# Another order for the last six down products of each batch, and a split end for the last store, in an AdaLN attention and LoRA-expert kernel

## What is computed

```python
g, u = xf @ Wg.T, xf @ Wu.T                       # 1024 x 704
base = silu(g) * u @ Wd.T                         # the base unit
for e in experts:                                 # rows outside the top two have weight 0
    h = silu(g + xf @ Ag_e.T @ Bg_e.T * 2) * (u + xf @ Au_e.T @ Bu_e.T * 2)
    acc += h @ Ad_e.T @ Bd_e.T * 2 * w_e
x = x + gb * (base + acc)
```

## Time and profile before

| | |
|---|---|
| median of 3 runs | 710.68 us (710.49 to 711.01) |
| profiled execution, its own time | 710.4 us |
| its span in the trace | 708.6 us |
| TensorE / VectorE / GpSimd / ScalarE busy | 94% / 72% / 55% / 48% |
| granted TensorE clock, mean | 0.992 |

### The profile page before, as it was taken

How to read it: one execution, slowest core, us unless ns; L and a number is a source line. 1 busy time by engine, 2 the same in 40 slices (tenths; PEclk the granted TensorE clock), 3 DMA queues, 4 the chain that set the end, 5 groups by cost and what they waited for, 6 DMA issues and landing times.

```text
span 708.6 us, 10697 instructions
## 1 busy us (share of the span) xinstructions
PE 665.5 (94%) x3760; PEld 561.0 (79%) x3760; DVE 509.1 (72%) x1152; ACT 340.2 (48%) x604; POOL 392.2 (55%) x518
## 2 busy tenths in 40 slices
PE   5879999999999999999999999999999999999995
PEld 3669977877789987877788897887778997788884
DVE  5996786688976778578986678677988669536323
ACT  4534354535355345454355436364445535454542
POOL 3794457537772257456774238554775245743644
PEclk9989999999999999999999999999999999999999
DMA  8400010000000010000000002000000000000000
GB/s 303 117 1 1 1 61 1 0 1 31 0 2 31 1 61 1 0 1 31 0 1 31 1 1 61 0 1 1 30 2 1 31 1 1 0 1 1 31 0 31
DMA packets 14037, 15.44 MB, mean 22 GB/s; under 512 B 1312, under 2 KB 12704, under 8 KB 13984
## 3 DMA queue, kind: packets, MB, share of 16 engines
q1 hardware_dynamic: 13984, 14.76, 6.4%
HBM read 10.57 MB, written 4.19 MB: 21 GB/s over the span
## 4 chain that ended last, share of the span: by engine, by line
PE 55%; DVE 28%; issue 9%; POOL 5%; ACT 2%; DMA 1%; POOLq 0%; SPq 0%; DVEq 0%; ACTq 0%
PE ps L1198 50%; PE ps L1207 5%; DVE hid L1068 4%; DVE zb L799 3%; DVE zb L817 3%; POOL ring_lo L441 2%; DVE zb L804 2%; DVE stat L814 1%; DVE tm_hi L1058 1%; DVE tm_lo L1058 1%; DVE xr L817 1%; DMA xs<-in_L_attn_x 1%; DVE onehot L1019 1%; DVE stat L951 1%; DVE mv L791 1%
## 5 line engine op out<-in xcount | busy, mean ns | idle before, releaser
L441 POOL TENSOR_TENSOR ring_lo<-hid,ring_hi 128x512 fp32r<-128x512 f32 x144 | 192.3, 1342 | 104.2 <-ACT ring_hi L684 103.4
L676 ACT ACTIVATE act_s<-ps 128x512 f32<-128x512 f32 x120 | 71.8, 599 | 150.3 <-PE ps L1198 150.3
L1068 DVE TENSOR_TENSOR hid<-act_s,ps 128x512 f32<-128x512 f32 x120 | 81.5, 681 | 78.7 <-ACT act_s L676 69.5
L684 ACT ACTIVATE ring_hi<-hid 128x512 fp32r<-128x512 f32 (+1 forms) x144 | 90.3, 627 | 18.9 <-DVE hid L1068 10.2
L429 POOL TENSOR_TENSOR xr<-xr,xs 128x256 f32<-128x256 f32 x32 | 23.4, 733 | 91.8 <-DVE xr L959 91.8
L1198 PE MATMUL ps<-wdT_hi,ring_hi 128*128 128x256 f32 x192 | 53.1, 282 | 0.0
L1198 PE MATMUL ps<-wdT_lo,ring_hi 128*128 128x256 f32 x192 | 52.5, 279 | 0.0
L1198 PE MATMUL ps<-xT_hi,wgT_hi 128*128 128x512 f32 x96 | 39.3, 409 | 8.1 <-DVE hid L1068 8.1
L631 ACT ACTIVATE pT_hi<-ps 128x512 fp32r<-128x512 f32 (+3 forms) x48 | 21.8, 488 | 47.8 <-PE ps L1207 47.5
L1198 PE MATMUL ps<-wdT_hi,ring_lo 128*128 128x256 f32 x160 | 44.6, 279 | 0.0
L1198 PE MATMUL ps<-tm_hi,bgT_hi 128*128 128x512 f32 x96 | 40.6, 423 | 3.4 <-DVE hid L1068 3.3
(11 more groups left out here) (219 smaller groups left out, 2074.6 us busy)
## 6 DMA issues: line engine op xcount, KB each, us to landing
xs<-in_L_attn_x SPq DMA_DIRECT2D x4, 1024.0 KB, 5.6
out<-xr SPq DMA_DIRECT2D x7, 512.0 KB, 2.9
s_mod<-in_L_wmod SPq DMA_DIRECT2D x1, 1024.0 KB, 8.8
s_qkvT<-in_L_attn_qkv SPq DMA_DIRECT2D x1, 768.0 KB, 10.5
s_wg<-in_L_ffn_Wg SPq DMA_DIRECT2D x1, 704.0 KB, 8.0
s_wu<-in_L_ffn_Wu SPq DMA_DIRECT2D x1, 704.0 KB, 9.4
s_wd<-in_L_ffn_Wd SPq DMA_DIRECT2D x1, 640.0 KB, 8.3
s_mod<-in_L_wmod SPq DMA_DIRECT2D x1, 512.0 KB, 6.8
```

What stands on the lines that cost most here:

```text
L441: pool.tensor_sub(ring[1][:, place(n), :], hid[:, n % HID, :], ring[0][:, place(n), :].bitcast(fp32)).then_inc(h_lo.sem, 1)
L676: nc.scalar.activation(act_s[:, n % 2, :], ps[:, 2 * (n % 2), :], ACT.Silu).then_inc(silu_ready.sem, 1)
L684: nc.scalar.activation(ring[0][p0:P, place(n), :], hid[p0:P, n % HID, :], ACT.Copy).then_inc(h_hi.sem, 1)
L1068: V.tensor_mul(hid[:, n % HID, :], act_s[:, n % 2, :], ps[:, 2 * (n % 2) + 1, :]).then_inc(h_ready.sem, 1)
```

## The change

Two edits. First, `down_order` gives the last group of the last chunk, in every batch, the order expert one, expert two, base. Before, it had base, expert one, expert two. The transposes of the next batch keep their position: ahead of the first and of the second of the six. Second, in the last batch only: the eighth tile of `xr` is added by VectorE and no longer by GpSimd, and the last four tiles are stored as two, one and one, where they were stored as two and two.

```diff
         def down_order(ci, g):
-            slots = (0, 1, 2) if ci or g else (1, 2, 0)
+            slots = (1, 2, 0) if (ci, g) in ((0, 0), (NC - 1, GROUPS - 1)) else (0, 1, 2)
...
-        LAST_PIECES = 2
+        LAST_PIECES = ((TC, TC + 1), (TC + 2,), (TC + 3,))
...
-                    n = TC // LAST_PIECES if last and ci == NC - 1 else TC
-                    for i in range(ci * TC, (ci + 1) * TC, n):
-                        sp.wait_ge(out_ready.sem, out_ready.at(b, i + n - 1))
+                    pieces = LAST_PIECES if last and ci == NC - 1 else (range(ci * TC, (ci + 1) * TC),)
+                    for piece in pieces:
+                        i, n = piece[0], len(piece)
+                        if last and i == NT - 1:
+                            sp.wait_ge(last_row, 1)
+                        else:
+                            sp.wait_ge(out_ready.sem, out_ready.at(b, i + n - 1))
...
-                out_rows(b, range(TC, NT))
+                out_rows(b, range(TC, NT - 1 if last else NT))
...
                         V.tensor_mul(y_gb[:, t % 2, :], ...).then_inc(y_scaled.sem, 1)
+                        if last and i == NT - 1:
+                            dve.wait_ge(y_scaled.sem, y_scaled.at(b, i))
+                            V.tensor_add(xr[:, i, :], xr[:, i, :], y_gb[:, t % 2, :]).then_inc(last_row, 1)
```

More of the change, by code:

```diff
@@ L196, in adaln_attention_moe_lora @@
         unwaited = sem("unwaited")
+        last_row = sem("last_row")
         def signal(name, per_batch, credit=0):
@@ L362, in body @@
                 for ci in range(NC):
-                    n = TC // LAST_PIECES if last and ci == NC - 1 else TC
-                    for i in range(ci * TC, (ci + 1) * TC, n):
-                        sp.wait_ge(out_ready.sem, out_ready.at(b, i + n - 1))
+                    pieces = LAST_PIECES if last and ci == NC - 1 else (range(ci * TC, (ci + 1) * TC),)
[5 more added lines that the diff above has]
+                            sp.wait_ge(out_ready.sem, out_ready.at(b, i + n - 1))
                         sp.dma_start(out[b, i * P:(i + n) * P, :].rearrange("(i p) d -> p i d", p=P), xr[:, i:i + n, :]).then_inc(stored, 16)
             batches(sp, body)
-            sp.wait_ge(stored, 16 + 16 * (NC * B + LAST_PIECES - 1))
+            sp.wait_ge(stored, 16 + 16 * (NC * B + len(LAST_PIECES) - 1))
         @block.gpsimd
```

## The result

The changed kernel takes 714.21 us (median of 5, 714.09 to 714.47) against 710.68 us: ratio 1.0048, 95% interval 1.0034 to 1.0063. It is slower by half a per cent. The forecast was 714.2 us.

What follows compares the result with a forecast made beforehand. TensorE, 94% busy and without slack at the seams, was taken as the bound; the end chain runs through other engines. +4.1 + 0.0 - 0.65 = +3.5 us gave a 714.2 us median, range 713.3 to 715.3.

Steps and rivals of the forecast that it cites:

- The seams: At the three passages to the next batch, TensorE stands still: +1.38 us each, +4.1 us together.
- the slow start in the middle of the queries: At 211.06 us queries waited for split inputs of the second half; coming later they no longer wait: -0.13 us.
- The first stall: Ahead of the second transposes, TensorE waits for VectorE's last two normalised tiles: 0.8 us, where 12 base matmuls ran.
- the second: Ahead of the last expert down, TensorE waits for ScalarE's stack: 0.7 us, where 8 base matmuls ran.
- The last batch: Order in the final batch: stack and TensorE arrive together, so the last expert down starts no sooner; gain 0.0 us.
- The end: Last tile and stores: last store issued 0.26 us sooner, landing 0.4 us shorter; -0.65 us.
- the line through two rows: Last store's landing: 2.9 us at 512 KB and 2.1 at 256 KB, so 1.7 estimated at 128 KB.
- held-up add: VectorE's add of the last tile taking 1.40 us, the worst of its kind, with no shorter landing: bound +0.6 us.
- A: Rival: the order pays in the last batch and is free between batches; 708.0 us, chance 0.02.
- B: Rival: the passages between batches absorb the stall fully; 710.0 us, chance 0.05.
- C: Rival: another engine's wait in the attention part absorbs half of the stall; 712.0 us, chance 0.09.
- D: Rival: shifted queries meet another engine's queue, each batch losing some 0.8 us more; 716.5 us, chance 0.07.

Runs made afterwards that it cites:

- the pair of runs with VectorE's low part: New adds and stores, VectorE making unit 35's low part in GpSimd's place in the last batch: old order 710.19 us, new order there 709.20 us.
- the order alone: Kernel before with only the new order of the last downs in all four batches, its adds and stores unchanged: 714.47 us, ratio 1.0055.
- the single-stores run: Kernel before with only the last two tiles stored singly, old order, all four last adds on GpSimd: 710.26 us, ratio 0.9997.

## Why the prediction was right

**The seams, 1.38 us each, 4.1 in all: right by its own steps.** The second transposes at their old time, the stack at its old time, the first query 1.51 us later, the slow start in the middle of the queries gone: each stands in the trace; the stretches grew by 1.41, 1.30 and 1.45. That the median came out at 714.21, 0.01 from the forecast, is luck: the profiled spans differ by 3.7 us and not 3.5, and single executions of a kernel scatter by 0.4 us and more. The step on which it rested, that nothing in ScalarE's order depends on what moved, is shown by the stack's time in the trace after, and by the run that moves it. That all of it arrives at the end is shown by the first up product, 4.16 us later beyond the 0.11 of the start.

The first stall was put at 0.8 us with work missing from it, the second at 0.7; recorded are 0.64 and 0.55, since the record counts the wait from the end of a matmul and I counted from where the next could have started. The sum did not go by them. But I had not seen that they are coupled: filling the first makes the second vanish as well, though the rows that tell it, the stack's end and the rates of the downs, were all in my sum.

**The last batch, 0.0 us: right for the wait, silent on the clock.** The stack and TensorE's arrival coincide, as read from 697.98 and 698.09; the pair of runs with VectorE's low part shows both bounds. What I left out was that the filled idle time can also keep the clock at 2.4 GHz. The profile of before did not show it, since its clock held. It is worth 0.5 us (6.76 against 6.25) in the executions in which the clock falls as late as in that trace, more than my bounds of 0.1; in the medians, 709.81 against 710.04, it is not told from nothing. It may be why the order alone cost 3.8 us in the medians while its three stretches grew by 4.0, and why the change cost 3.5 us in the medians and 3.7 in the profiled spans; that is not shown.

**The end, -0.65 us: right, 0.59 measured.** The last issue came 0.29 us sooner, counted from the first up product (4.02 against 4.31), where 0.26 was worked out, and 0.1 us after VectorE's add was done, as worked out. The landing took 1.8 us against 2.1, where the line through two rows gave 1.7. The Trainium skill (DMA: Bandwidth & Descriptors, Anatomy of one DMA) makes the half store 0.3 us shorter. The last store of the changed kernel agrees with that; the one of the single-stores run, 1.7 us, agrees with my line.

The forecast's range took -0.7 to -0.2 for the end, though the bound worked out for a held-up add was +0.6; with it the range would have reached higher. I read the earlier trace rows as a spread of 0.42 to 1.40 with a median of 0.91, but no product took 0.91: twelve took 0.42 to 0.43 us and twelve 1.40. Each of the slow twelve began while a GpSimd instruction had 1.1 us to go, and ended 0.3 us after it. One of them, in the trace of before (timeline):

```profile
182.62 1.47 POOL L441 TENSOR_TENSOR ring_lo<-hid,ring_hi 128x512 fp32r<-128x512 f32 x1
182.98 1.40 DVE L812 TENSOR_TENSOR gated<-zb,bc 128x256 f32<-128x256 f32 x1
```

In the changed kernel VectorE's add began 0.12 us before GpSimd's last one ended (707.52 + 2.09 = 709.61) and ended 0.31 us after it (709.92), having taken 0.43 us. So the +0.6 needed a long overlap, and the times in my own sum left only 0.14 us for one.

**The rivals.** A (708.0 us) fell with the run that has the order in the last batch alone. B and C (the seams absorb it) fell with the stretches. D (a larger loss in the attention part) did not occur: the gap between a seam's first query and the next seam's transposes was 159.38 us before (367.61 - 208.23) and 159.28 after (369.13 - 209.85).

## What to carry to other kernels

Work that depends on nothing is a cushion: ask of each piece that is moved behind a wait what stood in the wait's shadow until now, and at every place where the same rule applies, not only at the place that it is for. Here one condition on chunk and group moved 20 matmuls in all four batches; in three of them they were the cover of two waits, in the fourth they went into idle time, where they cost nothing.

Where two bounds end at the same time, taking either away gives nothing, and the row that shows their coincidence is worth more than both idle times; a version with both edits is then the one to run. Here that is the new order in the last batch alone together with VectorE's low part of the last unit, 709.20 us.

## What the runs showed of the hardware

Over an idle time of 2.96 us TensorE's granted clock fell from 2.4 to 1.2 GHz in the profiled executions of two kernels and held in those of three others with the same idle time. In the two it fell at different points, 0.9 us ahead of the next matmul and 0.2 us behind it, and the up products then ran 0.21 instead of 0.117 us apart. In the eight kernels with matmuls in that time, useful or not, it held. A single profile of a kernel with such a gap tells only one of its cases: the profile of before told the better one.

A VectorE product of two SBUF tiles that began with 1.1 us of a GpSimd instruction still to run took 1.40 us instead of 0.42. One that began 0.12 us before GpSimd's end lost nothing that can be seen (0.43 us).
